# A graph network's gather loop: POOL waits for its own third landing ahead of every second group of a ring lap

## The chip, the cores and the metric

The kernel runs on one core of a Trainium2 chip. The metric is the device time of one execution in microseconds. The core's engines are TensorE (PE), VectorE (DVE), ScalarE (ACT), GpSimd (POOL) and SyncE (SP), each with its own instruction queue; they meet through semaphores. Sixteen DMA engines move the data.

## The reference

A graph of 6250 nodes and 100,000 edges, sorted by destination. First four graph convolutions, then two layers of edge attention; features are 128 or 256 wide, everything in fp32.

```python
h = x @ W                                   # convolution, four times
out = segment_sum(h[src] * norm[:, None], dst) + b
# between them: gate, layer norm, elu

att = einsum('ehd,ehd->eh', q[dst], k[src]) / scale      # attention, two layers, 8 heads
ex = exp(clip(att) - max)
aggr = segment_sum(v[src] * alpha, dst)
x = x + aggr @ Wo + bo
x = x + gelu(layernorm(x) @ W1 + b1) @ W2 + b2
```

Self loops are added to the edges in both. The costly part is `h[src]` and `k[src]`, `v[src]`: a row of 512 bytes or 1 KB for each edge, in the order of the destinations.

## The kernel before

**Passes.** `p` runs over six passes, 0 to 3 the convolutions (`CONVS = 4`), 4 and 5 attention; the text counts the convolution passes from one. Each pass ends with a table of node rows in HBM (`tables[p + 1]`), which the next one gathers from. The rows (`WIDTH`) are 128 words wide in the first and the fourth pass, and 256 in the second and third and in both attention passes.

**Groups and the ring.** The edges are cut into columns of 128, four columns are a group (`GC = 4`), and seven groups are a lap of the ring (`RG = 7`, 28 slots, `RING`). A convolution pass gathers 112 groups (16 laps), because the ten tiles of nodes with the most edges are done by dense multiplication with an adjacency matrix that is built at the start; an attention pass gathers all 196 groups (28 laps). In all there are 840 groups and 3360 gathers.

**POOL** runs `gather_lap`. For each group `q` of a lap it waits until the ring's place is free (`groups_freed`), then issues four indirect DMAs at L1449. Each gathers 128 rows, one for each partition, into its slot, and increments the slot's semaphore `landed[j]` by 16 at its landing. After group 3 it copies the next lap's indices (`stage`, L1434). Before any group but the first of a lap it also waits until the third of the four gathers of the group before it has landed; that is the wait which the change touches. `slots_seen` and `staging_seen` are only incremented.

**SP** waits for the four landings of each group in order and increments `group_landed` (L1356 in the convolutions, L1389 in attention). In attention it also loads a row of destinations for each group, 256 KB, two groups ahead.

**The consumers.** In the convolutions PE multiplies a mask that DVE makes (L807) with the gathered rows (L1969), tile by tile, and works on the dense tiles between them (L1949, L1934), whose adjacency parts ACT loads. A group is free when DVE has seen PE's masks used (L864, L874). In attention PE spreads `q` over the edges (L1864), DVE multiplies it with the gathered `k` (L1024), reduces, clips, and after ACT's exponential (L1577) multiplies with the gathered `v` (L1044); PE adds the messages up (L1873), and ACT frees the group (L1584). Each pair of node tiles is followed by its own chain of norms and small matrix products.

What sets the order is the queues: nothing is planned at run time, and each engine takes its own instructions in the order in which they are written.

Of the kernel before, what the change touches and what calls it, by code (L numbers as in the profile page):

```python
# [56 lines left out]
def build_gnn(nc, w, out):  # L57
# [84 lines left out]
    with ExitStack() as ctx:  # L142
# [1255 lines left out]
        def _(pool):  # L1398
# [33 lines left out]
            def stage(half, col):  # L1432

                pool.tensor_copy(idx_stage[:, half, :], src_idx[:, bass.ds(col, RING)]).then_inc(idx_staged, 1)  # L1434

            def gather_lap(p, lap, half, staged, ahead_col):

                for q in range(RG):
                    if q == 0:
                        pool.wait_ge(idx_staged, staged + 1)  # L1440
                        pool.sem_inc(staging_seen, 1)

                    if q > 0:
                        pool.wait_ge(landed[q * GC - 2], lap * 16 + 16)
                        pool.sem_inc(slots_seen, 1)
                    pool.wait_ge(groups_freed, lap * RG + q + 1)
                    pool.sem_inc(slots_seen, 1)
                    for j in range(q * GC, (q + 1) * GC):
                        pool.indirect_dma_start(  # L1449
                            ring[:, j, 0:WIDTH[p]], None, tables[p][:, :],  # L1450
                            bass.IndirectOffsetOnAxis(ap=idx_stage[:, half, j:j + 1], axis=0),
                        ).then_inc(landed[j], 16)
                    if q == RG // 2:


                        pool.wait_ge(group_landed, lap * RG + 1)
                        pool.sem_inc(staging_seen, 1)
                        stage(1 - half, ahead_col)
# [6 lines left out]
            for p in range(CONVS):  # L1465


                pool.wait_ge(rows_written, 16 * stores_before(p))
                if p > 0:
                    pool.sem_inc(groups_freed, 2)  # L1470
                    pool.wait_ge(idx_staged, p * (2 * laps + 1))
                    pool.sem_inc(staging_seen, 1)
                stage(0, lap_col(0))
                with pool.Fori(0, laps) as two:
                    for half in range(2):
                        lap = two * 2 + half
                        gather_lap(p, p * 2 * laps + lap, half, p * (2 * laps + 1) + lap, lap_col(lap + 1))
            for p in range(CONVS, PASSES):


                pool.wait_ge(rows_written, 16 * stores_before(p))
                if p == CONVS:
                    pool.sem_inc(groups_freed, 2)
                before = CONVS * (2 * laps + 1) + (p - CONVS) * (LAPS * sweeps + 1)
                pool.wait_ge(idx_staged, before)
                pool.sem_inc(staging_seen, 1)
                stage(0, 0)
                with pool.Fori(0, sweeps) as s:
                    with pool.Fori(0, LAPS // 2) as two:
                        for half in range(2):  # L1490
                            lap = two * 2 + half
                            gather_lap(p, CONVS * 2 * laps + ((p - CONVS) * sweeps + s) * LAPS + lap, half,
                                       before + s * LAPS + lap, (lap + 1) * RING)
# [729 lines left out]
```

## Time and profile before

| | us |
|---|---|
| median of 3 runs | 6797.37 (6784.47 to 6805.76) |
| the profiled execution, its own time | 6788.08 |
| its span | 6786.3 |
| POOL busy | 3378.6 (50%) |
| PE busy | 4680.9 (69%) |
| DVE busy | 3844.6 (57%) |
| mean granted TensorE clock | 0.812 |

The span goes from the first instruction to the last of the profiled execution. The first 819 us prepare degrees, ranges and the adjacency; the convolution passes begin their gathers at 819, 1589, 2357 and 3140 us, the attention passes at 3871 and 5344 us. In the rows below a line such as L1449 is a line of the kernel; "<-" names what ended a wait, "issue" is time in which the engine waited for nothing that the profile shows.

### The profile page before, as it was taken

What the parts mean: (1) busy time and instruction counts of PE and PEld (TensorE: products, weight loads), DVE (VectorE), ACT (ScalarE), POOL (GpSimd) and SP (SyncE); (2) the same over time, 40 slices, a digit from 0 to 9 for tenths busy, and PEclk for the clock granted to TensorE, in tenths of its full rate; (3) what the DMA queues carried; (4) which work ended last, traced back from release to release, by engine and by line L of the source; (5) the groups of instructions that cost most, each with busy time, mean ns of one, the idle gap of its engine ahead of it and who ended that gap; (6) DMA issues with size and microseconds to landing.
All of it is one profiled execution on the core that took longest, in us unless ns stands there. A gap on an engine that the chain in (4) does not pass through costs nothing.

```text
span 6786.3 us, 115362 instructions
## 1 busy us (share of the span) xinstructions
PE 4680.9 (69%) x24609; PEld 3667.0 (54%) x24740; DVE 3844.6 (57%) x10619; ACT 676.7 (10%) x1598; POOL 3378.6 (50%) x3512
## 2 busy tenths in 40 slices
PE   2577666667789788887577566666677666666666
PEld 1111255556677567776555345555566445555555
DVE  8644446773444424443344555666767556676676
ACT  0011100000000000100000100011122200111111
POOL 0000066664655466554666566666544366666442
PEclk9856677778999899998788688788888788888777
DMA  1011232323444344433233244443333244444332
GB/s 49 19 57 57 106 98 88 103 85 113 122 132 142 106 130 123 132 110 119 81 103 103 65 120 120 122 123 116 107 103 105 74 122 122 119 123 121 103 101 61
DMA packets 308327, 696.19 MB, mean 103 GB/s; under 512 B 68879, under 2 KB 118156, under 8 KB 306822
## 3 DMA queue, kind: packets, MB, share of 16 engines
q0 software_dynamic: 146944, 381.90, 20.1%
q10 hardware_dynamic: 94620, 196.31, 8.5%
q1 hardware_dynamic: 66538, 115.35, 5.6%
q8 instruction: 97, 1.59, 0.1%
q14 instruction: 128, 1.05, 0.0%
HBM read 625.45 MB, written 67.83 MB: 102 GB/s over the span
## 4 chain that ended last, share of the span: by engine, by line
PE 30%; issue 18%; DVE 16%; DMA 16%; POOL 12%; DVEq 7%; POOLq 1%; SPq 0%; ACT 0%; ACTq 0%
DMA ring<-rows,idx_stage 15%; POOL ring L1449 12%; PE acc_ps L1969 7%; PE bank L1949 4%; PE acc_ps L1873 3%; PE q_ps L1864 2%; PE bank L2011 2%; PE bank L1934 2%; DVE even_rows L601 1%; PE bank L2123 1%; DVE dots L1027 1%; DVE wide L1024 1%; DVE msg L1044 1%; DVEq L729 1%; PE bank L2151 1%
## 5 line engine op out<-in xcount | busy, mean ns | idle before, releaser
L1449 POOL DMA_INDIRECT ring<-rows,idx_stage x3360 | 3336.0, 993 | 2261.4 <-DMA ring<-rows,idx_stage 1006.1
L1969 PE MATMUL acc_ps<-ring,masks 128*128 x4800 | 1041.8, 369 | 469.5 <-SPq L1356 304.6
L807 DVE SCALAR_TENSOR_TENSOR masks<-dst_f,neg_first,lane 128x256 f32<-128x256 f32 x1200 | 545.3, 483 | 1209.7 <-PE acc_ps L1969 1078.5
L1969 PEld LDWEIGHTS acc_ps<-ring,masks 128*128 128x128 f32 x4800 | 847.2, 220 | 612.5 <-issue 547.0
L1873 PE MATMUL acc_ps<-msg,masks 128*128 x3904 | 724.2, 342 | 502.7 <-DVE msg L1044 502.5
L1873 PEld LDWEIGHTS acc_ps<-msg,masks 128*128 128x128 f32 x3904 | 636.8, 239 | 605.0 <-issue 601.4
L1864 PE MATMUL q_ps<-odd_rows,conv_only 128*128 (+1 forms) x3904 | 636.1, 320 | 393.7 <-DVE conv_only L814 387.1
L1864 PEld LDWEIGHTS q_ps<-odd_rows,conv_only 128*128 128x128 f32 x3904 | 570.2, 227 | 441.5 <-issue 433.5
L1434 POOL COPY idx_stage<-src_idx 128x28 int32 (+1 forms) x126 | 36.5, 289 | 1058.3 <-DVE turn_b L748 809.8
L1024 DVE TENSOR_TENSOR wide<-q_ps,ring 128x512 f32 x392 | 270.5, 690 | 336.5 <-SPq L1389 288.5
L814 DVE TENSOR_SCALAR conv_only<-conv_only,node_id 128x512 f32 x488 | 236.5, 497 | 346.5 <-PE q_ps L1864 215.0
L835 DVE SCALAR_TENSOR_TENSOR masks<-dst_f,neg_first,lane 128x512 f32<-128x512 f32 x488 | 366.2, 750 | 98.7 <-PE acc_ps L1873 77.3
L729 DVE TENSOR_SCALAR ring<-ring 128x784 f16 x434 | 184.0, 424 | 316.5 <-PE q_ps L1835 110.0
L1027 DVE TENSOR_REDUCE dots<-wide 128x32 f32<-128x512 f32 x392 | 268.9, 686 | 13.3
L1044 DVE TENSOR_TENSOR msg<-ring,msg x392 | 268.6, 685 | 1.0 <-ACT msg L1577 0.6
L1577 ACT ACTIVATE msg<-logits x392 | 89.1, 227 | 1756.6 <-DVE logits L1035 1735.6
L601 DVE TENSOR_TENSOR even_rows<-lane_bf,even_rows 128x1024 bf16<-128x1024 bf16 x196 | 238.7, 1218 | 29.2 <-PE bank L1800 18.3
L1800 PE MATMUL bank<-even_rows 128*128 128x49 bf16 x1568 | 91.2, 210 | 226.2 <-DVE even_rows L603 225.9
L2011 PE MATMUL bank<-conv_only,wide 128*128 128x256 f32 x490 | 181.1, 494 | 87.8 <-DVE rows L998 87.8
L1845 PE MATMUL q_ps<-bias_rows,zeros_bf 128*128 128x512 bf16 x520 | 151.0, 418 | 95.6 <-DVE wide L1024 85.9
L1745 ACT ACTIVATE wide<-q_ps 128x512 f32<-128x512 f32 (+2 forms) x75 | 38.9, 519 | 1685.3 <-PE q_ps L1849 1685.3
L1800 PEld LDWEIGHTS bank<-even_rows 128*128 128x128 bf16 x1568 | 70.3, 112 | 249.9 <-DVE even_rows L603 249.1
(304 smaller groups left out, 6263.1 us busy)
## 6 DMA issues: line engine op xcount, KB each, us to landing
conv_only<-dst_rows SPq DMA_DIRECT2D x396, 256.0 KB, 3.4
ring<-rows,idx_stage POOLq DMA_INDIRECT x3360, 2.8
adjacency<-odd_rows ACTq DMA_DIRECT2D x10, 3136.0 KB, 8.9
conv_only<-adjacency ACTq DMA_DIRECT2D x70, 384.0 KB, 3.7
msg<-adjacency ACTq DMA_DIRECT2D x60, 384.0 KB
wide<-adjacency ACTq DMA_DIRECT2D x60, 384.0 KB, 3.7
turn_b<-adjacency ACTq DMA_DIRECT2D x60, 384.0 KB
part<-adjacency ACTq DMA_DIRECT2D x30, 448.0 KB, 3.9
```

The costliest lines, as they stand in the source:

```text
L601: vec.tensor_tensor(one_lo[:, j0:j1, :], lane_bf[:, :].unsqueeze(1).broadcast_to([P, k, P]), lo_f[:, e, bass.ds(b * HC + j0, k)].unsqueeze ...
L807: return vec.scalar_tensor_tensor(out=to, in0=dst_f[:, bass.ds(col + 2 * h, 2)].unsqueeze(2).broadcast_to([P, 2, P]), scalar=neg_first[:, ...
L835: vec.scalar_tensor_tensor(out=to, in0=dst_f[:, bass.ds(col, GC)].unsqueeze(2).broadcast_to([P, GC, P]), scalar=neg_first[:, bass.ds(t, 1) ...
L1024: vec.tensor_tensor(qk[:, :, :], q_ps[:, k, :].rearrange("p a (c f) -> p (a c) f", f=D), ring[:, bass.ds(slot, GC), 0:D], ALU.mult).then_i ...
L1027: vec.tensor_reduce(dots[:, :, :], qk[:, :, :].rearrange("p c (h d) -> p c h d", h=H), AX_X, ALU.add).then_inc(edge_step, 1)
L1044: vec.tensor_tensor(msg[:, k, :, 0:D].rearrange("p a c (h d) -> p (a c) h d", h=H), ring[:, bass.ds(slot, GC), D:KV].rearrange("p c (h d) ...
L1449: pool.indirect_dma_start(ring[:, j, 0:WIDTH[p]], None, tables[p][:, :], bass.IndirectOffsetOnAxis(ap=idx_stage[:, half, j:j + 1], axis=0) ...
L1864: ins = pe.matmul(to, mask_t[:, u, j, :], q_rows[:, bass.ds(t + u, 1), :].rearrange("p a f -> p (a f)"), start=u == 0, stop=u == nxt)
L1873: ins = pe.matmul(acc(t, 0, MSG), masks[:, 1 if shared else 0, j, :], msg[:, bass.ds(g & 1, 1), j, :].rearrange("p a m -> p (a m)"), start ...
L1949: ins = pe.matmul(to, parts(p)[q % PART_RING][:, r * P:(r + 1) * P], rows_in[p][:, m, 0:WIDTH[p]], start=False, stop=m == TILES - 1)
L1969: ins = pe.matmul(to, masks[:, u, j, :], rhs, start=False, stop=final and j == GC - 1)
L2011: pe.matmul(to, pair_t[:, i * K + k, :], conv_w[p][:, k, :], start=k == 0, stop=False)
```

## The change

POOL's wait for the third landing of the preceding group stands ahead of groups 1, 3 and 5 of each lap, and no longer ahead of groups 2, 4 and 6. Group 0 has none before or after. The semaphore increment beside it goes with it. Everything else stays.

```diff
@@ -1440,7 +1440,7 @@
                         pool.wait_ge(idx_staged, staged + 1)
                         pool.sem_inc(staging_seen, 1)
 
-                    if q > 0:
+                    if q % 2 == 1:
                         pool.wait_ge(landed[q * GC - 2], lap * 16 + 16)
                         pool.sem_inc(slots_seen, 1)
                     pool.wait_ge(groups_freed, lap * RG + q + 1)
```

## Rows read from the trace of the kernel before

**Rows 1.** The page: busy time by engine, and the group of L1449.
```profile
PE 4680.9 (69%) x24609; PEld 3667.0 (54%) x24740; DVE 3844.6 (57%) x10619; ACT 676.7 (10%) x1598; POOL 3378.6 (50%) x3512
...
L1449 POOL DMA_INDIRECT ring<-rows,idx_stage x3360 | 3336.0, 993 | 2261.4 <-DMA ring<-rows,idx_stage 1006.1
```

**Rows 2.** Table of waits, whole span: us in total, times, longest us.
```profile
POOL ring L1449 <- DMA ring<-rows,idx_stage: 1006.1, 575, 5.5
...
POOL ring L1449 <- ACTq L1584: 304.4, 82, 9.8
```

**Rows 3.** Chain of waits, shares by line, for eight stretches in order of time.
```profile
by line: issue 17.7%; POOL ring L1449 15.9%; DMA ring<-rows,idx_stage 12.3%; PE acc_ps L1969 8.7%; DVE even_rows L601 4.0%; PE bank L1949 3.4%; PE bank L2011 3.2%; DVEq L481 3.2%; DVE masks L807 3.1%; DVE even_rows L603 2.6%; PE bank L1934 
...
by line: PE acc_ps L1969 23.3%; PE bank L1949 13.4%; DMA ring<-rows,idx_stage 10.2%; issue 9.8%; POOL ring L1449 8.0%; PE bank L1934 6.7%; PE bank L2011 5.8%; PE q_ps L1849 2.7%; DVEq L481 2.7%; DVE rows L991 2.0%; PE acc_ps L1925 1.8%; DVE
...
by line: PE acc_ps L1969 26.8%; PE bank L1949 17.1%; issue 8.0%; PE bank L2011 7.2%; DMA ring<-rows,idx_stage 5.5%; PE bank L1934 4.5%; POOL ring L1449 4.2%; PE bank L2021 3.6%; PE q_ps L1849 3.3%; DVE rows L991 2.1%; DVE masks L807 1.6%; P
...
by line: DMA ring<-rows,idx_stage 28.9%; POOL ring L1449 25.1%; issue 24.1%; PE acc_ps L1969 3.6%; DMA conv_only<-adjacency 3.2%; PE bank L2064 2.0%; PE q_ps L1934 1.8%; PE q_ps L1949 1.3%; DVE masks L807 0.7%; DVEq L481 0.6%; PE bank L1849
...
by line: DMA ring<-rows,idx_stage 37.9%; POOL ring L1449 26.3%; issue 25.4%; PE acc_ps L1873 1.4%; DVE wide L1024 1.0%; DVE dots L1027 1.0%; DVE msg L1044 0.7%; PE q_ps L1864 0.6%; POOLq L1446 0.5%; DVE masks L835 0.4%; PE bank L2151 0.4%; 
...
by line: issue 18.6%; DMA ring<-rows,idx_stage 10.6%; PE acc_ps L1873 9.2%; POOL ring L1449 7.4%; PE q_ps L1864 6.5%; PE bank L2123 3.5%; DVE dots L1027 3.4%; DVE wide L1024 3.3%; PE bank L2151 3.2%; DVE msg L1044 2.8%; PE bank L1849 1.9%; 
...
by line: DMA ring<-rows,idx_stage 38.8%; POOL ring L1449 26.3%; issue 25.1%; PE acc_ps L1873 1.8%; DVE wide L1024 0.8%; DVE dots L1027 0.8%; DVE msg L1044 0.8%; POOLq L1446 0.6%; PE q_ps L1864 0.6%; PE bank L2151 0.4%; PE bank L2123 0.3%; D
...
by line: issue 15.6%; PE acc_ps L1873 12.7%; PE q_ps L1864 8.4%; DMA ring<-rows,idx_stage 5.5%; PE bank L2123 5.3%; DVE wide L1024 4.0%; DVE dots L1027 4.0%; DVE msg L1044 4.0%; POOL ring L1449 4.0%; PE bank L2151 3.6%; DVE stats L1135 1.7%
```

**Rows 4.** Table of waits: 3140 to 3871, 1589 to 2357, 3871 to 4450.
```profile
PE acc_ps L1969 <- SPq L1356: 194.9, 67, 5.9
...
PE acc_ps L1969 <- SPq L1356: 30.7, 12, 4.2
...
DVE wide L1024 <- SPq L1389: 141.1, 60, 4.3
```

**Rows 5.** Busy time by stretch: PE, PEld, DVE, ACT, POOL, then PEclk, DMA, GB/s.
```profile
1589.00:2357.00 768.00, 643.62 (x2752) 521.07 (x2751) 329.55 (x980) 45.76 (x75) 439.96 (x465) 0.93 0.42 128
...
3140.00:3871.00 731.00, 478.71 (x2621) 394.11 (x2621) 312.08 (x1181) 57.72 (x173) 437.52 (x465) 0.78 0.33 98
```

**Rows 6.** Timeline of POOL, fourth pass: start us, us, idle before it.
```profile
3318.24 0.94 POOL L1449 DMA_INDIRECT ring<-rows,idx_stage  x1 [1.22 <-DMA ring<-rows,idx_stage]
...
3323.33 0.94 POOL L1449 DMA_INDIRECT ring<-rows,idx_stage  x1 [0.30 <-issue]
3324.58 0.95 POOL L1449 DMA_INDIRECT ring<-rows,idx_stage  x1 [0.30 <-issue]
...
3329.26 0.94 POOL L1449 DMA_INDIRECT ring<-rows,idx_stage  x1 [1.24 <-DMA ring<-rows,idx_stage]
...
3335.47 0.94 POOL L1449 DMA_INDIRECT ring<-rows,idx_stage  x1 [1.51 <-DMA ring<-rows,idx_stage]
...
3341.40 0.94 POOL L1449 DMA_INDIRECT ring<-rows,idx_stage  x1 [1.24 <-DMA ring<-rows,idx_stage]
```

**Rows 7.** Timeline of POOL, first attention pass, first gathers of five groups.
```profile
4081.26 0.97 POOL L1449 DMA_INDIRECT ring<-rows,idx_stage  x1 [1.24 <-DMA ring<-rows,idx_stage]
...
4087.64 0.94 POOL L1449 DMA_INDIRECT ring<-rows,idx_stage  x1 [1.28 <-DMA ring<-rows,idx_stage]
...
4094.23 0.94 POOL L1449 DMA_INDIRECT ring<-rows,idx_stage  x1 [1.89 <-DMA ring<-rows,idx_stage]
...
4099.34 0.94 POOL L1449 DMA_INDIRECT ring<-rows,idx_stage  x1 [0.30 <-issue]
...
4106.80 0.95 POOL L1449 DMA_INDIRECT ring<-rows,idx_stage  x1 [2.76 <-issue]
```

**Rows 8.** L1449's landings, third convolution pass, then first attention pass.
```profile
DMA to landing us min/median/max: 2.7/2.8/5.8
...
DMA to landing us min/median/max: 2.7/3.0/4.8
```

## The prediction

> **What bounds the kernel now.** I read the page's costliest groups first, since the change touches one line of one engine. POOL is busy for only half the span, but its gather line L1449 has 2261 us of idle time in front of it, and the largest named share of it, 1006 us, ended with a landing of one of its own gathers [rows 1]. The reader should see an engine that waits for itself: it issues three gathers, and cannot go on until the third is back. The table of waits gives the count: 575 such waits of 1.75 us on average, beside 304 us in 82 waits for a free group (ACT, L1584) [rows 2]. So POOL is stopped by the ring being full only now and then.
>
> Idle time matters only where it is on the path, so I cut the chain of waits into eight stretches: the four convolution passes, and each attention pass split where its chain changes character [rows 3]. Gathers in flight ("DMA ring") and POOL's own issue ("POOL ring") carry over half the chain in the fourth convolution pass, and 64 and 65% of it in the first 580 us of each attention pass. In the first three convolution passes and the second halves of the attention passes they carry 28, 18, 10, 18 and 10%. There PE or DVE lead. The consumers tell the same: in 3140 to 3871 PE waits 195 us in 67 waits for a landed group, in 1589 to 2357 only 31 us in 12; DVE's first attention step waits 141 us in 60 waits for one in 3871 to 4450 [rows 4]. PE's granted clock is 0.93 in the second pass and 0.78 in the fourth [rows 5]: it is lower where PE stands and waits more.
>
> **What one removed wait gives.** Four gathers cost POOL about 5.0 us (0.94 us each and 0.30 us between them). With the wait, the next group starts 1.2 to 1.5 us after the last issue instead of 0.3. The trace of before already holds the changed code: the first group of each lap has no such wait. In the fourth pass the group at 3323.33 is such a one. From 3318.24 to 3329.26, one group without and one with the wait take 11.02 us; from 3329.26 to 3341.40, two groups with it take 12.14 us [rows 6]. One wait less is worth 1.12 us.
>
> In attention the same pairs give 4094.23 to 4106.80, 12.57 us, against 4081.26 to 4094.23, 12.97 us [rows 7]: only 0.40 us. The gap behind the unwaited group is 2.76 us there. POOL ran ahead by some 1.2 us, and then stood for nearly as long more. A 256 KB destination row is loaded beside each group in attention, and a gather's landing is there a median of 3.0 us behind its issue, in the third convolution pass, whose rows are equally wide, 2.8 us [rows 8]. I read it as the third gather meeting that load when POOL comes earlier. The Trainium skill ("DMA: Bandwidth & Descriptors", the section on queues, rings and completion order) says that each DMA engine takes its queues in turn, a whole packet at a time, which speaks against running further ahead; by a full giveback of that kind the attention passes would gain nothing, and by none they would gain as the convolutions do. These rows lie between: 0.40 of 1.12.
>
> **The change part by part.** It removes three of a lap's six waits: ahead of groups 2, 4 and 6. It adds nothing and moves nothing past another queue; the number and order of gathers, of SP's loads and of ACT's loads stay. The semaphore increment beside each removed wait goes too. The unwaited group at 3323.33 still waits for a free group and increments a semaphore, and its first gather starts 0.30 us behind the last one, as the next within the group does [rows 6]; so such a pair of steps costs nothing that a row shows, and I put it at nothing. Behind the waiting instruction on POOL stand the next group's four gathers and, once a lap, the index copy; who waits for those is SP (the group's four landings), and behind SP, PE or DVE. So what comes earlier is each landing.
>
> How many waits lie on the path: each puts one gather in flight on the chain, so the "DMA ring" share of a stretch times its length, by 2.8 us (convolution) or 3.0 us (attention) a landing, counts them. Passes one to four: 12.3% of 770, 10.2% of 768, 5.5% of 783 and 28.9% of 731 us give 34, 28, 15 and 75; attention 37.9% of 579, 10.6% of 894, 38.8% of 576 and 5.5% of 866 us give 73, 32, 74 and 16. Half are removed: 76 in the convolutions, 98 in attention.
>
> Convolutions: 76 x 1.12 = 85 us. In attention a lap now has one run without waits (the first group). After, it has three: group 2, group 4, and groups 6 and 0 together. The giveback comes once a run. Runs of one are worth 0.40 each; the double run is worth the single one's 0.40 and a whole saving of some 1.25 more, of which 0.40 is there already. That makes 0.40 + 0.40 + 1.25 = 2.05 us for three removed waits, 0.68 each: 98 x 0.68 = 67 us. Sum 152 us.
>
> The bounds. Upper: the mean wait is 1.75 us and not the typical one of my rows; without it 0.30 stays, so 1.45 us each, 174 x 1.45 = 252 us. Lower: in the stretches with small shares, the saved time may end at PE or DVE after a few groups; without those (63 waits of the 174) 38 x 1.12 + 74 x 0.68 = 93 us stay. If the giveback of attention fell on every removed wait, it is 38 x 1.12 + 74 x 0.40 = 72 us. I take the row prices for all, as the long waits left out above and the stretches counted in full pull to opposite sides. The profiled execution took 6788.1 us (span 6786.3); less 152 it is 6636. The median of the runs shown lies 9.3 us above it, so I say 6645.
>
> **Rivals.**
> *The consumers are the limit anyway.* POOL arrives earlier, the ring of seven groups fills, and the stall turns into waits for a free group. For it: the small chain shares in five of eight stretches, and POOL's 82 waits for a free group. Against: 195 and twice 141 us of starved PE and DVE, which no ring fills by itself. It would give less than 20 us: 6778 to 6797, no measurable change (0.3%, 20 us, is about what a measurement of this kernel can tell).
> *The change isn't felt by POOL*, since the wait that is left collects the delay of the removed one: landings, not issues, set the pace. For it, attention's 0.40 of 1.12; against, 1.12 in the fourth pass. If all of attention returned its gain and the convolutions kept theirs, 6797 - 85 = 6712.
> *Slower: a deep run of gathers stalls.* Groups 5, 6 and 0 come as twelve gathers without a wait, where before at most eight did. The longest landing in the third pass is 5.8 us, that is four or five gathers in flight at 1.25 us apiece; no row shows more. Should POOL or the DMA queues stall once a lap beyond that, it would appear as long idle ahead of group 0's gathers or as issues well over 0.94 us. 174 removed waits are 58 laps on the path, worth 152/58 = 2.6 us a lap; a stall of more than 3.0 us a lap makes the kernel measurably slower. At 5 us a lap: 58 x 2.4 = 139 us more, 6936.
>
> **How the numbers follow.** Gain of 50 us or more, with the waits on the path: 0.74. Consumers the limit: 0.10. That only the convolutions keep theirs is the high side of this case, 0.10 of those 0.74. Stall: 0.09. A gain above 252 us, by PE's clock rising towards the second pass's 0.93 in the fourth pass and the long waits being removed too: 0.07. So faster 0.80, same 0.11, slower 0.09. The likeliest case alone spans 6545 (252 us) to 6725 (72 us). The range of 8 in 10 is 6540 to 6785: it leaves out the stall, most of the no-change case, and the very large gain.
>
> **What the changed profile would show.** POOL's waits for its own landings near 290 in place of 575, and their sum from 1006 to some 550 us or less, as the remaining ones are longer in attention (2.5 to 3 us). Waits for ACT L1584 up from 304 us, because the ring is full sooner. Groups 2, 4, 6 and 0 about 5.1 us behind the group before them. PE's 195 us for L1356 down by 40 to 50, DVE's 141 us for L1389 down by 25 to 40 in each attention pass. The fourth pass shorter by some 43 us, each first 580 us of attention by 25 to 40, the second pass by 10 to 20. The prediction is wrong if the issues at L1449 get longer than 0.94 us in the run over groups 5, 6 and 0, if the remaining waits grow by as much as the removed ones held, or if PE's clock in the second pass falls below its 0.93.

## The result and the profile after

The changed kernel took 6584.07 us (median of 4 runs, 6582.64 to 6585.87) against 6792.65 us (4 runs, 6784.47 to 6805.76): a ratio of 0.9691, 95% interval 0.9674 to 0.9708, so 3.1% faster. I had said 6645. (The table ahead of the prediction holds three of these four runs of before.) The profiled execution took 6583.14 us (span 6581.3), 204.9 us less than the one of before. In two later measurements, on two chips, the same edit made the kernel 4 to 5% slower; the experiments below are mostly about that.

The page of after, to be held against [rows 1]:

```profile
PE 4586.1 (70%) x24609; PEld 3599.2 (55%) x24740; DVE 3848.9 (58%) x10619; ACT 676.0 (10%) x1598; POOL 3377.1 (51%) x3512
...
L1449 POOL DMA_INDIRECT ring<-rows,idx_stage x3360 | 3338.2, 994 | 2048.3 <-issue 900.5
```

POOL does the same work in the same time: 3360 gathers at 994 ns. The idle time in front of them fell from 2261 to 2048 us. PE has as many instructions as before and is busy for 95 us less. The table of waits, against [rows 2]:

```profile
POOL ring L1449 <- issue: 900.5, 2899, 2.6
POOL ring L1449 <- DMA ring<-rows,idx_stage: 552.6, 277, 5.9
POOL ring L1449 <- ACTq L1584: 407.5, 109, 9.7
```

Half of the waits for an own landing are gone, 575 to 277, and with them 454 us of waiting. Of that, 103 us come back as waits for ACT to free a group (304 to 407). Busy time by stretch, passes two and four, against [rows 5], and the chain of waits of pass four, against the fourth of [rows 3]:

```profile
1562.00:2316.00 754.00, 644.18 (x2751) 522.49 (x2750) 328.53 (x978) 45.75 (x75) 442.20 (x465) 0.92 0.43 130
...
3073.00:3749.00 676.00, 452.66 (x2621) 377.40 (x2621) 311.78 (x1181) 57.34 (x173) 438.04 (x465) 0.82 0.35 106
```

```profile
by line: POOL ring L1449 37.8%; issue 27.7%; DMA ring<-rows,idx_stage 21.3%; PE acc_ps L1969 2.4%; PE bank L2064 1.3%; PE q_ps L1949 0.9%; POOL idx_stage L1434 0.5%; POOLq L1446 0.5%; PE bank L1849 0.4%; DVEq L481 0.4%; PE bank L2065 0.4%; 
```

Pass four is still POOL's: landings in flight fell from 28.9 to 21.3% of its chain, and POOL's own issue rose from 25.1 to 37.8%. Lengths of the passes, from first gather to first gather, in three kernels that come up here (us):

| pass | before | after | slow pace (below) |
|---|---|---|---|
| 1, 2, 3, 4 (convolution) | 770.6, 768.0, 783.2, 730.5 | 743.1, 754.3, 756.6, 676.1 | 909.3, 901.3, 902.8, 868.1 |
| 5, 6 (attention) | 1473.0, 1442.2 | 1434.6, 1397.7 | 1591.7, 1585.6 |

The convolutions give 122.2 us, attention 82.9. The timeline of POOL, one lap and the start of the next in pass four:

```profile
3256.02 0.94 POOL L1449 DMA_INDIRECT ring<-rows,idx_stage  x1 [1.19 <-DMA ring<-rows,idx_stage]
...
3261.28 0.97 POOL L1449 DMA_INDIRECT ring<-rows,idx_stage  x1 [0.16 <-issue]
...
3267.23 0.94 POOL L1449 DMA_INDIRECT ring<-rows,idx_stage  x1 [1.23 <-DMA ring<-rows,idx_stage]
...
3272.45 0.94 POOL L1449 DMA_INDIRECT ring<-rows,idx_stage  x1 [0.30 <-issue]
...
3277.44 1.03 POOL L1449 DMA_INDIRECT ring<-rows,idx_stage  x1 [0.31 <-issue]
...
3283.84 0.96 POOL L1449 DMA_INDIRECT ring<-rows,idx_stage  x1 [1.30 <-DMA ring<-rows,idx_stage]
```

These are the first gathers of groups 3, 4, 5, 6, 0 and 1. Groups 4, 6 and 0 start 0.16 to 0.31 us behind the last issue; groups 3, 5 and 1 wait about as long as they did before. The twelve gathers of groups 5, 6 and 0, from 3267.23 to 3282.53, run at 0.94 to 1.21 us each, with no stall.

### The profile page after: what moved, and what is told of

Read it like the earlier page. It is cut to its first block, busy times and chain, and to the rows that moved or that the text cites. A ratio compares the mean times of both kernels' runs of the same rounds, so it can differ in the third digit from the quotient of the medians.

```text
span 6581.3 us, 115002 instructions
## 1 busy us (share of the span) xinstructions
PE 4586.1 (70%) x24609; PEld 3599.2 (55%) x24740; DVE 3848.9 (58%) x10619; ACT 676.0 (10%) x1598; POOL 3377.1 (51%) x3512
## 4 chain that ended last, share of the span: by engine, by line
PE 31%; DVE 19%; issue 18%; POOL 14%; DMA 8%; DVEq 8%; POOLq 0%; SPq 0%; ACT 0%; ACTq 0%
POOL ring L1449 14%; DMA ring<-rows,idx_stage 8%; PE acc_ps L1969 7%; PE bank L1949 4%; PE acc_ps L1873 4%; PE q_ps L1864 2%; PE bank L2011 2%; PE bank L1934 2%; DVE even_rows L601 2%; DVE dots L1027 1%; DVE wide L1024 1%; PE bank L2123 1%; DVE msg L1044 1%; DVEq L729 1%; PE bank L2151 1%
## 5 line engine op out<-in xcount | busy, mean ns | idle before, releaser
L1449 POOL DMA_INDIRECT ring<-rows,idx_stage x3360 | 3338.2, 994 | 2048.3 <-issue 900.5
L1969 PE MATMUL acc_ps<-ring,masks 128*128 x4800 | 1020.3, 363 | 386.1 <-SPq L1356 233.1
L1969 PEld LDWEIGHTS acc_ps<-ring,masks 128*128 128x128 f32 x4800 | 831.4, 216 | 526.1 <-issue 462.5
L1873 PE MATMUL acc_ps<-msg,masks 128*128 x3904 | 708.1, 336 | 481.6 <-DVE msg L1044 481.1
L1873 PEld LDWEIGHTS acc_ps<-msg,masks 128*128 128x128 f32 x3904 | 625.6, 235 | 575.8 <-issue 571.2
L1864 PE MATMUL q_ps<-odd_rows,conv_only 128*128 (+1 forms) x3904 | 621.9, 315 | 392.0 <-DVE conv_only L814 385.9
L1864 PEld LDWEIGHTS q_ps<-odd_rows,conv_only 128*128 128x128 f32 x3904 | 557.3, 222 | 439.0 <-issue 430.6
L814 DVE TENSOR_SCALAR conv_only<-conv_only,node_id 128x512 f32 x488 | 235.9, 496 | 342.7 <-PE q_ps L1864 215.2
L835 DVE SCALAR_TENSOR_TENSOR masks<-dst_f,neg_first,lane 128x512 f32<-128x512 f32 x488 | 366.9, 752 | 106.2 <-PE acc_ps L1873 85.6
L1577 ACT ACTIVATE msg<-logits x392 | 89.1, 227 | 1677.4 <-DVE logits L1035 1638.8
```

The source lines that it names most:

```text
L835: vec.scalar_tensor_tensor(out=to, in0=dst_f[:, bass.ds(col, GC)].unsqueeze(2).broadcast_to([P, GC, P]), scalar=neg_first[:, bass.ds(t, 1) ...
L1449: pool.indirect_dma_start(ring[:, j, 0:WIDTH[p]], None, tables[p][:, :], bass.IndirectOffsetOnAxis(ap=idx_stage[:, half, j:j + 1], axis=0) ...
L1864: ins = pe.matmul(to, mask_t[:, u, j, :], q_rows[:, bass.ds(t + u, 1), :].rearrange("p a f -> p (a f)"), start=u == 0, stop=u == nxt)
L1873: ins = pe.matmul(acc(t, 0, MSG), masks[:, 1 if shared else 0, j, :], msg[:, bass.ds(g & 1, 1), j, :].rearrange("p a m -> p (a m)"), start ...
L1969: ins = pe.matmul(to, masks[:, u, j, :], rhs, start=False, stop=final and j == GC - 1)
```

## The experiments

**Series one: which half pays.** One chip; four kernels that differ only in the condition of the wait.

```diff
-                    if q % 2 == 1:                             # the change
+                    if (q % 2 == 1 if p < CONVS else q > 0):   # conv_only
+                    if (q > 0 if p < CONVS else q % 2 == 1):   # attn_only
+                    if q in (1, 2, 3):                         # deep_run: groups 4, 5, 6 and 0 without
+                    if False:                                  # no_wait: none at all
```

> The change in the four convolution passes alone (q % 2 == 1 for p < CONVS), the attention passes as before. By pass starts, the changed kernel's convolutions are 122 us shorter and its attention passes 83 us. Theory A (each wait puts a landing on POOL's own chain, and what it gives is local to its pass): the two parts add up, so this kernel takes 6792.7 - 122 = 6670 us, give or take 10, with convolution passes as long as in the changed kernel and attention passes as long as before. Theory B (a common cause outside the waits, such as a higher TensorE clock all over): the attention passes get shorter too, and the time is below 6650.

> The change in the two attention passes alone. Theory A: 6792.7 - 83 = 6710 us, give or take 10; the saved times of this and of the convolutions-only kernel add up to the whole 208. Theory B: they do not add up by 20 us or more. Full giveback in attention, the rival on record: nothing below 6780.

> Waits ahead of groups 1, 2 and 3 only: as many waits as in the changed kernel, but groups 3 to 6 and group 0 of the next lap come as one run of 20 gathers without a wait instead of at most 12. Theory A with a giveback once for each run: same as the changed kernel in the convolutions, and in attention two givebacks fewer a lap on some 32 laps on the path, some 0.5 us each, 30 us: 6550 to 6590. Stall theory (a deep run of gathers stalls POOL or the DMA queues): above 6600, with issues at L1449 over 0.95 us or long idle without a releaser inside the run.

> None of the waits for a third landing is left; POOL waits only for a free group. Theory A: the remaining waits are 277 of 2.0 us, about 175 of them on the chain by its DMA share; at 1.2 us each, which is what the first half gave, 208 us go, less what PE and DVE keep as they become the limit: 6400 us, between 6370 and 6480. Consumers-are-the-limit theory: 6560 or more, with POOL's waits for a free group up by all that the landing waits lose. Stall theory: slower than the changed kernel.

Measured, as ratios to the kernel before on that chip (6922.38 us): change in the convolutions alone 1.026 (1.023 to 1.029), in attention alone 1.020 (1.018 to 1.022), three waits left but all in one run 1.053 (1.051 to 1.055), none left 1.066 (1.064 to 1.068). All are slower, which nothing in the first two traces explains. The kernels with more and longer runs of gathers without a pause lose more. And the kernel before itself was 1.9% slower than in the first measurement. So I ran the changed kernel itself again.

**Series two: the same kernels on another chip.** after_again is the changed kernel, before_again the one before, the two others are copies of series one.

> The changed kernel itself, beside the kernel before on one chip. The four kernels of the first series took 2 to 7% more than the kernel before in pairs on their chip, against 3.1% less for the changed kernel, which lies between them in its waits. If the waits' price is the same everywhere, this gives 0.969 again, and the parts of the change are slower for a reason of their own. If what a removed wait brings depends on the chip or the state that it meets, the ratio is above 1 here where the kernel before takes 6920 us, and 0.97 where it takes 6790.

> The kernel before itself, for a trace of the same chip as the changed kernel beside it. Same condition as in the first trace: 6790 us and nearly no stretch in which PE, DVE and ACT all stand still. The other condition: 6920 us, with stretches of some 5 us in which all three stand still at once, as in the kernel without waits.

> The kernel without any of the waits, beside the changed kernel on one chip. Theory A: 6400 us, between 6370 and 6480, and below the changed kernel. If the loss of the first series belongs to the kernel (gathers in a deep run bring all engines to a stop), it is above the changed kernel wherever it runs, by some 500 to 800 us.

> The change in the convolution passes alone, once more. By the changed kernel's pass starts 6670 us and a ratio of 0.982. In the condition of the first series: 1.026.

Before took 6994.24 us there (6947.72 to 7043.63); the change 1.0491 (1.042 to 1.056), no wait 1.065 (1.058 to 1.072), convolutions alone 1.026 (1.018 to 1.034). The finding of the first series repeats, and the changed kernel, 3.1% faster in the first measurement, is 4.9% slower on this chip. Where the time goes is seen in the changed kernel's timeline, first attention pass:

```profile
4318.47 1.15 PE L1864 MATMUL q_ps<-odd_rows,conv_only 128*128 128x128 f32 x8
...
4321.10 0.75 DVE L835 SCALAR_TENSOR_TENSOR masks<-dst_f,neg_first,lane 128x512 f32<-128x512 f32 x1 [1.57 <-remote]
4321.34 0.23 ACT L1577 ACTIVATE msg<-logits  x1 [5.26 <-remote]
...
4322.80 1.19 PE L1873 MATMUL acc_ps<-msg,masks 128*128 x8 [2.10 <-DVE msg L1044]
...
4324.24 0.95 POOL L1449 DMA_INDIRECT ring<-rows,idx_stage  x1 [0.30 <-issue]
4326.67 0.95 POOL L1449 DMA_INDIRECT ring<-rows,idx_stage  x1 [1.48 <-issue]
...
4328.69 0.49 DVE L814 TENSOR_SCALAR conv_only<-conv_only,node_id 128x512 f32 x1 [6.23 <-remote]
...
4329.51 0.79 PE L1864 MATMUL q_ps<-odd_rows,conv_only 128*128 128x128 f32 x2 [5.52 <-issue]
```

POOL goes on gathering while DVE, ACT and PE all stand, DVE for 6.2 us. "Remote" is a releaser that the view of the trace does not name. What DVE waits for ahead of L814 can be found in the trace's records of semaphores. It is `q_ready` (L827), which PE's last matmul of L1864 increments. That matmul has ended by 4319.6, but the increment is recorded at 4328.15, and PE runs nothing from 4324.0 until then. DVE's wait at L827 ends at 4328.17 and SP's wait for the same semaphore (L1383) at 4328.16. So SP, which has nothing for 8.75 us there, is not late: it waits for PE's increment as DVE does. ACT's 5.26 us have the same end: the increment of PE's matmul of L1873 that DVE's masks (L835) and ACT (L1577) wait for is recorded at 4320.93, 2.6 us behind the end of that matmul.

This is no single case. The end of a matmul in the trace is modelled, but where the records are whole, PE's increments stand 0.01 to 0.02 us behind it. The table counts from 815 us on. A standstill is a stretch of over 1.5 us in which PE, DVE and ACT run no instruction; the next two columns say how much of it ended with an increment of SP's and of PE's. The last two columns are PE's increments recorded more than 0.5 us behind the end of the last matmul that could have made them, and SP's slow steps, which come up below.

| run | standstill, us | ended by SP | by PE | late increments of PE | slow SP steps |
|---|---|---|---|---|---|
| before | 277 | 174 | 0 | 0 of 3192 | 0 |
| after | 244 | 139 | 0 | 0 of 3195 | 0 |
| paced_slow (below) | 613 | 515 | 0 | 0 of 3194 | 0 |
| before_again | 428 | 61 | 237 | 809 of 2755 | 269 |
| after_again | 746 | 3 | 624 | 1050 of 2801 | 328 |
| no_wait | 733 | 9 | 492 | 1132 of 2816 | 354 |
| after_third (below) | 717 | 7 | 581 | 1041 of 2809 | 298 |
| delay (below) | 353 | 137 | 108 | 584 of 2687 | 240 |

The difference in standstill between before_again and after_again, 318 us, is as large as the 310 us between their spans. In the first two traces the engines stand mostly for SP, which forwards the landings of gathers. On these chips they stand mostly for PE's increments, and every increment of PE's that ended a standstill there was a late one. The lateness follows the density of the gathers: of PE's recorded increments in before_again 14% are late with three gathers issued in the 6 us ahead of the matmul's end, 43% with four and 81% with five; in after_again 17, 60 and 90%.

The table of waits of before_again and then of after_again:

```profile
POOL ring L1449 <- ACTq L1584: 508.3, 131, 13.0
POOL ring L1449 <- DMA ring<-rows,idx_stage: 411.1, 188, 5.5
POOL ring L1449 <- DVEq L874: 167.7, 47, 18.5
```

```profile
POOL ring L1449 <- ACTq L1584: 861.3, 203, 11.7
POOL ring L1449 <- DVEq L874: 447.1, 97, 24.0
...
POOL ring L1449 <- DMA ring<-rows,idx_stage: 163.2, 69, 5.9
```

POOL arrives early and then waits for free groups: 861 us at L1584 against 508.

Two more things set these traces apart, both counted from their records. SP's own steps (register and semaphore instructions), which take 0.01 to 0.18 us in the first two traces, take 0.6 to 0.8 us 269 times in before_again, 328 in after_again and 394 in no_wait_again, and never in the first two; a few dozen of DVE's do too. These do not show that SP works late. The record of a step of SP's that increments a semaphore stands over 0.2 us behind the increment itself, by 0.7 us in the median, in 219 of 1226 cases in before_again and 231 of 1259 in after_again, and in none in before. So at least part of the stretching is in the records.

And the semaphore increments are not all there. From 819 us on the first trace of before holds 13 to 16 a microsecond, that of after 14 to 16; before_again holds 6 to 7, after_again 5 to 7, although the preparation ahead of 819 us shows the same rate in all (3.2 and 2.0 in its halves). Most of the missing ones are those of landings: after_again has 26,233 increments by DMA engines, after 68,162. The records of DMA packets are whole in both, 308,340 each. The slow steps follow the density of the gathers too: of SP's steps in before_again 2% are slow with three gathers issued in the 6 us ahead, 8% with four, 10% with five; in after_again 3, 12 and 18%.

**Series three: is it the wait, or its pause?** On the chip of series one. after_third is the changed kernel. delay leaves the waits out as the change does, and lets POOL do four small memsets of a tile that nobody reads in their place. The change has turned `if q > 0:` into `if q % 2 == 1:`, so the `elif` below means groups 2, 4 and 6. paced has no wait for a landing, and one memset behind every gather.

```diff
+                    elif q > 0:                                # delay
+                        for k in range(4):
+                            pool.wait_ge(idled, lap * 12 + (q // 2 - 1) * 4 + k + 1)
+                            pool.sem_inc(slots_seen, 1)
+                            pool.memset(idle_tile[:, :], 0.0).then_inc(idled, 1)
...
+                        pool.wait_ge(idled, lap * RING + j + 1)          # paced
+                        pool.sem_inc(slots_seen, 1)
+                        pool.memset(idle_tile[:, :], 0.0).then_inc(idled, 1)
```

> The changed kernel a third time, as the yardstick of this series. Complete records of landings and a kernel before of 6790 us: ratio 0.969. Records mostly missing, SP's register and move instructions taking 0.7 us by the hundred where they take 0.03, and a kernel before of 6920 to 7010 us: ratio near 1.05.

> The changed kernel with POOL kept busy ahead of groups 2, 4 and 6 by four small memsets in turn (about 0.3 us each, 1.2 us in all) where the waits for the third landing were. It sets the same pace as the kernel before, but does not wait for any landing there. Rate theory (what costs, in the condition with slow SP instructions, is how many gathers are issued in some 6 us): ratio 1.00, between 0.99 and 1.015. Theory that the wait for the landing itself is what protects: as the changed kernel beside it, 1.05. In the condition of the first traces it gives back the gain: 0.99 to 1.005.

> No wait for a third landing at all; a small memset of POOL behind each gather instead, so that gathers come evenly, some 1.55 us apart, 6.2 us a group, never five in 6 us. Rate theory: as good as the kernel before or better, 0.985 to 1.005, since the double runs at the lap's end are gone too; far below the kernel without waits, which took 1.066. Wait theory: 1.05 or more, as no landing is awaited. In the condition of the first traces: 0.98 to 1.00.

Before took 6932.37 us; the change 1.043 (1.040 to 1.047), nearly the sum of its two halves in series one on this chip; delay 1.0075 (1.005 to 1.010), paced 1.048 (1.045 to 1.051). The timeline of POOL in delay:

```profile
4306.72 0.95 POOL L1456 DMA_INDIRECT ring<-rows,idx_stage  x1 [0.30 <-issue]
4307.66 0.22 POOL L1452 MEMSET idle_tile<- 128x128 f32 x1
4308.03 0.20 POOL L1452 MEMSET idle_tile<- 128x128 f32 x1 [0.15 <-issue]
4308.39 0.20 POOL L1452 MEMSET idle_tile<- 128x128 f32 x1 [0.15 <-issue]
4308.75 0.20 POOL L1452 MEMSET idle_tile<- 128x128 f32 x1 [0.15 <-issue]
4309.59 0.95 POOL L1456 DMA_INDIRECT ring<-rows,idx_stage  x1 [0.64 <-issue]
```

A pause of 1.9 us that awaits no landing takes back most of the loss: 1.043 to 1.0075, standstill from 717 to 353 us, PE's late increments from 1041 to 584, slow SP steps from 298 to 240, and 47,978 increments recorded in place of 41,628. So on these chips it needs no awaited landing to avoid most of the loss. It does not follow that only the spacing counts. The pause is longer than the wait that it stands for (a median of 1.94 us ahead of groups 2, 4 and 6, against 1.51 us in the first trace of before), and from the third gather of a group to the first of the next it is 4.3 us. A landing comes a median of 2.8 us behind its issue, so behind such a pause the third gather has mostly landed anyway. A shorter pause, which would tell the two apart, was not run.

paced was mis-sized by me: its memset fell mostly into the 0.30 us that lie between two gathers anyway, so they came 1.34 us apart and not the 1.55 expected, 5.35 us a group. With 1.048 it lies between the changed kernel (1.043) and the one without waits (1.066 in series one) and tells nothing about a true pace.

**The last run: a true pace, by the same means.** No wait for a landing, and two memsets behind each of the first three gathers of a group.

```diff
+                        if j % GC < GC - 1:
+                            for k in range(2):
+                                pool.wait_ge(idled, lap * (RG * 6) + q * 6 + (j % GC) * 2 + k + 1)
+                                pool.sem_inc(slots_seen, 1)
+                                pool.memset(idle_tile[:, :], 0.0).then_inc(idled, 1)
```

> No wait for an own landing at all, as in the kernel without any; behind the first, second and third gather of each group POOL does two small memsets, each waiting for the one before, so that a gather starts 1.55 to 1.75 us behind the one before it within a group and a group takes POOL some 6.0 to 6.5 us, about what the kernel before spends on one with its wait. The memsets write a tile that nothing reads. Under the condition of the study's other runs (SyncE's own steps of 0.7 us in the trace): if what costs is how densely the gathers follow each other, the time is within -1.0 to +1.5% of the kernel before (ratio 0.990 to 1.015), stretches in which PE, DVE and ACT all stand still come to 200 to 300 us and not 476 to 613. If it is the missing wait for the landing itself that costs, the time is as without any wait: ratio 1.05 to 1.066, with over 450 us stood still. Under the condition of the first two traces (complete landing records): 0.99 to 1.00, by either.

It came to a chip that is neither of these two, where before took 6791.92 us (7 runs, 6775.45 to 6797.18), as in the first measurement. Its time was 7576.65 us, 1.116 (1.114 to 1.118). I had expected 0.99 to 1.00 there. POOL's timeline, and the chain of waits from 3300 to 3900 us, over the third and fourth pass:

```profile
3308.21 0.95 POOL L1448 DMA_INDIRECT ring<-rows,idx_stage  x1 [0.48 <-POOL idle_tile L1456]
3309.16 0.22 POOL L1456 MEMSET idle_tile<- 128x128 f32 x1
3309.54 0.20 POOL L1456 MEMSET idle_tile<- 128x128 f32 x1 [0.15 <-POOL idle_tile L1456]
3310.22 0.95 POOL L1448 DMA_INDIRECT ring<-rows,idx_stage  x1 [0.48 <-POOL idle_tile L1456]
```

```profile
by line: POOL ring L1448 39.1%; issue 32.3%; POOL idle_tile L1456 16.0%; POOLq L1454 2.0%; POOLq L1455 1.2%; PE acc_ps L1973 1.2%; PE bank L2015 1.0%; DMA ring<-rows,idx_stage 0.9%; PE bank L2025 0.7%; POOLq L1445 0.5%; DVE rows L992 0.4%; 
```

Again the size was wrong: the pair costs 0.76 us and not the 0.3 to 0.5 expected, since a memset that waits for another starts 0.15 us behind it and the gather 0.48 us behind the last. A gather comes 2.01 us after the one before, and a group every 7.42 us (median) where before needs 6.38. So it cannot answer what I ran it for; the bounds on standing still in its expectation were counted in another way than the table above and are not to be held against it. It shows two other things. Where the records are whole (this trace has 13 to 15 increments a microsecond, no slow step of SP and no late increment of PE), POOL's pace becomes the kernel's: 1.04 us a group times 840 groups is 874 us, and 791.7 us of it arrive in the span. And its fourth pass, 868.1 us, is 112 x 7.42 = 831 us of gathers and a tail of 37.

## Why the prediction was right, step by step

**The sign and the path: right.** POOL's own waits were on the path in part of the kernel, and half of them went. Own-landing waits near 290 and at most some 550 us: 277 and 552.6. The waits that are left grew little, from 1.75 to 2.0 us on average. L1584 up: 304 to 407. Groups 2, 4, 6 and 0 about 5.1 us behind the one before: medians 5.25, 5.36, 5.21 and 5.21, the excess being single issues of 1.1 to 1.2 us. The fourth pass shorter by 43: 54.4. The second by 10 to 20: 13.7. PE's 195 us at L1356 in pass four [rows 4] down by 40 to 50, and DVE's 141 us at L1389 by 25 to 40 in each attention pass; the rows of after for pass four and the first 561 us of pass five:

```profile
PE acc_ps L1969 <- SPq L1356: 148.6, 58, 5.7
...
DVE wide L1024 <- SPq L1389: 99.0, 56, 4.5
```

They are 46 and 42 us less, and the second attention pass has 95.9 us in place of 140.4, so DVE's waits fell a little more than forecast. Two of the three signs of being wrong were badly chosen. Three of the twelve issues of the long run took 1.03 to 1.21 us, but 600 of the 3360 take over 1 us in the trace of before too, and the median stayed 0.95. And the granted clock of the second pass did fall below 0.93, to 0.92 [rows 5], while the pass became 13.7 us shorter.

That the measured sign was the forecast one was in part luck: nothing in the prediction says that it could depend on the condition which the chip is in.

**The sum: 152 said, 205 measured.** The convolution term, 76 x 1.12 = 85, was mis-sized; it measured 122. By pass it was 34, 28, 15 and 75 waits, half of them at 1.12: 19, 16, 8 and 42 us; measured 27.5, 13.7, 26.6 and 54.4. The excess is in the first, third and fourth. Of the first pass I had said that PE or DVE lead; its chain has POOL's gathers as the largest line [rows 3]. In the fourth, the 15 laps between the first gathers of laps one and sixteen take 606.3 us in place of 654.0: 47.7 us for 45 removed waits, 1.06 each. So the price was right, and the count too low: on average all of the removed waits paid, 48 in that pass, where I counted 37.5 from the chain's share of landings. In the third pass, where PE leads the chain, PE is busy for 659.2 us in place of 673.9 at a granted clock of 0.95 instead of 0.93: 15 of the 26.6 us. The rows of before and of after:

```profile
2357.00:3140.00 783.00, 673.91 (x3080) 555.42 (x3078) 335.68 (x995) 60.51 (x100) 439.30 (x465) 0.93 0.39 118
...
2316.00:3073.00 757.00, 659.19 (x3079) 544.02 (x3078) 336.59 (x995) 60.48 (x100) 440.67 (x466) 0.95 0.41 122
```

I had left the clock out of the sum and given it to a rival. That PE's shorter work is what shortened that pass was read from the rows and tested by no run.

**The attention term: 67 said, 82.9 measured.** The giveback is there, but smaller where POOL leads. The first 88 groups of the two attention passes took 533 and 539 us in place of 577 and 578, 44 and 39 us less (25 to 40 said), and that is the whole 82.9: behind them one pass lost 6 us and the other gained 6. My sum had 50 us in the first stretches and 16 in the second ones. It was too low in the first, and the second, where PE and DVE lead, gave nothing, as my lower bound had it for them. In the first attention pass, POOL waits 2.19 and 2.09 us behind a single group without a wait (first and last row), and 2.64 us behind two (second row), where the trace of before showed 2.76 behind a single one [rows 7]:

```profile
3951.26 0.94 POOL L1449 DMA_INDIRECT ring<-rows,idx_stage  x1 [2.19 <-DMA ring<-rows,idx_stage]
...
3969.03 0.94 POOL L1449 DMA_INDIRECT ring<-rows,idx_stage  x1 [2.64 <-DMA ring<-rows,idx_stage]
...
3980.91 0.94 POOL L1449 DMA_INDIRECT ring<-rows,idx_stage  x1 [2.09 <-DMA ring<-rows,idx_stage]
```

At the start of that pass four laps (28 groups), from first gather to first gather, took 169.8 us in place of 182.3: 3.1 us a lap against my 2.05. I had taken one pair of rows, and it was a poor one. What the giveback is was tested by no run: that the third gather meets the load of the destination row stays a reading.

**The rivals.** Consumers the limit: false in the first measurement as a whole, true of the later stretches of attention. A deep run of gathers that stalls POOL or the DMA queues: the issues at L1449 last as long as before (median 0.95 us, 99 in 100 under 1.47 us, in the traces of before, of after and of no_wait alike), so as I put it it is false. I had also read the longest landing as 5.8 us, from the third pass alone; in the trace of before landings of other passes reach 6.8 us. The outcome of that rival, slower, is nevertheless what two of the three measurements of the change gave (+4.3 and +4.9%): where gathers are dense, PE's increments come late. I had looked for the stall on POOL's queue and not on the engine whose increments the others wait for.

**What is settled and what is open.** Shown: with the same edit the time falls by 3.1% in one condition and rises by 4.3 and 4.9% in another. In the second, the added standstill ends with late increments of PE's; a pause without any awaited landing restores most of it. For the gain itself the evidence is the lengths of the passes and the rows. The two runs that were to split it, conv_only and attn_only, met the other condition, so that the gain is POOL's waits in the fourth pass, and partly the clock in the third, is read from the traces.

Not shown: what makes a chip be in the second condition, and what holds PE's increments back. On which chip the first measurement ran is not known, so it is not settled either that the condition belongs to the chip and not to the time. One reading is that the recording itself does it. All timed executions here carry their records, so none is free of it. The traces fit: on the two chips 5 to 8 increments a microsecond are kept where 14 to 16 are made, more are kept when gathers are spaced (delay), and SP's records lag behind its increments. The Trainium skill ("NOTIFIC — the notification-queue block", section "Overflow: three behaviours, one of which stalls the engine") says that a queue of records whose ring is full drops the new one, overwrites the oldest or stalls the producer, by its setting, and that the block's internal pipeline always presses back on the producers rather than lose a record. The missing increments and PE's late ones are what that could look like; no run here shows the kernel without records on such a chip, so the +4 to +5% may belong to the measurement and not to the kernel.

The other reading, that these chips land gathers more slowly by themselves, finds no support in the records: the 397 gathers of after_again with all sixteen increments recorded landed a median of 2.81 us behind their issue, 3239 of after 2.84 us. As most gathers of after_again have no whole record, this speaks against that reading without excluding it.

## What to carry to other kernels

Where an engine waits for its own transfer, ask whether the wait is worth its landing or only its pause: replace it by a fixed pause, shorter than the landing takes, and see. The chain's share of landings counted too few of the waits that paid where POOL leads, and too many where PE and DVE lead in attention; the clock that a less starved TensorE gets belongs in the sum. When several engines stand, look for the semaphore that ends the wait and for the engine that increments it, before the one that also stands is blamed. And look into a trace for missing landings and stretched steps before an effect of a few per cent is believed on one chip: the same edit had both signs here.

## What was unexpected in the hardware

- The kernel before took 6792 us in two chip visits and 6922 to 6994 us in three others, without overlap (single runs at most 6806 and at least 6911.8).
- In the latter (two of them on one chip), PE's increments were recorded more than 0.5 us behind the end of their matmul in 584 (delay) to 1153 (no_wait_again) of some 2700 to 2800 cases, and in the standstills the engines that waited for them started only then; in the three traces of the faster visits in none of 3192 to 3195. With three, four and five gathers issued in the 6 us ahead, 14, 43 and 81% were late in before_again.
- There, SP's steps of 0.01 to 0.18 us took 0.6 to 0.8 us some 240 to 394 times an execution, and its records stood by 0.7 us behind increments that it had already made.
- A memset of 128x128 on POOL took 0.20 to 0.22 us; two chained by a semaphore start 0.36 to 0.38 us apart, and one behind a gather hides almost whole in the 0.30 us ahead of the next (1.34 us from gather to gather instead of 1.25).
- Twelve gathers in a row, and with no wait at all more, left the time of one issue as it was (means of 993 ns in before, 994 in after, 991 in no_wait).
